# Decoder layer on one core: score maxima and exponentials of two chunks by one instruction across two PSUM banks

## The reference

```python
def xattn(q, ctx):                       # q: (2, 512, 128), ctx: (2, 154, 128)
    qh, kh, vh = heads(q @ Wq + bq), heads(ctx @ Wk + bk), heads(ctx @ Wv + bv)
    logits = einsum('bhqd,bhkd->bhqk', qh, kh) / sqrt(8)
    i, j = arange(512)[:, None], arange(154)[None, :]
    b = (i >= j - 154 + 512)             # query i sees key j only if i >= j + 358
    logits = logits * b - 1e10 * (1 - b)
    return merge(softmax(logits) @ vh) @ Wo + bo
x = layernorm(x + linear_attention(x))
x = layernorm(x + xattn(x, ctx))
x = layernorm(x + expert_ffn(x))
```

## Time and profile before

| | |
|---|---|
| median of 3 runs | 153.23 us (152.84 to 153.42) |
| the profiled execution | 153.2 us |
| its span, first to last instruction | 151.1 us |
| TensorE busy | 139.0 us (92%) |
| VectorE busy | 98.1 us (65%) |
| ScalarE busy | 93.2 us (62%) |
| GpSimd busy | 76.4 us (51%) |
| TensorE's mean granted clock | 0.970 of full speed |

### The profile page before, as it was taken

One profiled execution on the slowest core, in us unless ns is written; L12 is line 12 of the kernel. 1 busy time (PEld: TensorE's weight loads), 2 busy tenths in 40 slices (PEclk: granted clock), 3 DMA queues, 4 the chain that ended last, 5 costly groups with the idle time before them and its releaser, 6 DMA issues.

```text
span 151.1 us, 2620 instructions
## 1 busy us (share of the span) xinstructions
PE 139.0 (92%) x856; PEld 99.4 (66%) x856; DVE 98.1 (65%) x278; ACT 93.2 (62%) x185; POOL 76.4 (51%) x123
## 2 busy tenths in 40 slices
PE   7999998999999699999799599999999999999950
PEld 2679775656666357577468378876887888888620
DVE  0388898989369500556686775774468866776974
ACT  3276635995943542479866766656567566676761
POOL 8600994489349990003453546654365566654000
PEclk9999999999999955999999999999999999999996
DMA  4839984000000000360143033400843345300013
GB/s 119 247 66 297 359 307 153 0 4 4 0 0 4 0 4 8 108 169 25 46 148 127 7 139 131 121 26 25 265 131 116 105 135 128 127 28 0 2 42 97
DMA packets 9625, 14.44 MB, mean 96 GB/s; under 512 B 1662, under 2 KB 4718, under 8 KB 9356
## 3 DMA queue, kind: packets, MB, share of 16 engines
q1 hardware_dynamic: 9324, 13.75, 29.4%
q10 hardware_dynamic: 288, 0.52, 0.9%
HBM read 13.69 MB, written 0.59 MB: 94 GB/s over the span
## 4 chain that ended last, share of the span: by engine, by line
PE 44%; DVE 15%; issue 15%; POOL 13%; DMA 5%; ACT 4%; POOLq 1%; DVEq 0%; ACTq 0%
POOL ek L826 13%; DMA pT<-comb_d 4%; PE bank L428 4%; PE bank L662 3%; PE bank L664 3%; PE bank L663 3%; PE bank L338 3%; PE bank L345 3%; DVE bank L1080 2%; PE bank L481 2%; DVE alo L1086 2%; PE bank L546 2%; PE bank L520 2%; DVE y L898 2%; PE bank L675 2%
## 5 line engine op out<-in xcount | busy, mean ns | idle before, releaser
L826 POOL TENSOR_TENSOR ek<-ek,pT 128x512 f32<-128x512 f32 x30 | 38.7, 1291 | 43.1 <-ACT ek L1119 40.8
L1080 DVE SCALAR_TENSOR_TENSOR bank<-bank,b_sb,ek 128x512 f32<-128x512 f32 x34 | 25.7, 757 | 20.8 <-POOL ek L826 19.2
L1119 ACT ACTIVATE ek<-bank,b_sb 128x512 f32<-128x512 f32 x34 | 23.4, 688 | 15.4 <-PE bank L664 15.3
L662 PE MATMUL bank<-x2hi,w1hi 128*128 128x512 f32 x68 | 27.8, 409 | 3.1 <-DVE alo L1086 3.1
L1119 ACT ACTIVATE stacks<-bank,mult_sb 128x512 fp32r<-128x512 f32 x34 | 23.4, 687 | 7.1 <-DVE bank L1080 5.9
L664 PE MATMUL bank<-x2hi,w1lo 128*128 128x512 f32 x68 | 26.8, 394 | 0.0
L663 PE MATMUL bank<-x2lo,w1hi 128*128 128x512 f32 x68 | 26.7, 392 | 0.0
L1086 DVE SCALAR_TENSOR_TENSOR alo<-bank,mult_sb,stacks 128x512 fp32r<-128x512 f32 x34 | 25.3, 743 | 1.0 <-ACT stacks L1119 0.9
L662 PEld LDWEIGHTS bank<-x2hi,w1hi 128*128 128x128 f32 x68 | 12.8, 188 | 9.0 <-DVE alo L1086 5.0
L664 PEld LDWEIGHTS bank<-x2hi,w1lo 128*128 128x128 f32 x68 | 12.8, 188 | 3.0
L663 PEld LDWEIGHTS bank<-x2lo,w1hi 128*128 128x128 f32 x68 | 12.8, 188 | 2.5
(11 more groups left out here) (189 smaller groups left out, 236.3 us busy)
## 6 DMA issues: line engine op xcount, KB each, us to landing
pT<-comb_d SPq DMA_DIRECT2D x30, 256.0 KB, 3.2
early<-w1T_d SPq DMA_DIRECT2D x1, 1536.0 KB, 7.7
late<-w2T_d SPq DMA_DIRECT2D x1, 1088.0 KB, 5.4
early<-w1T_d SPq DMA_DIRECT2D x1, 640.0 KB, 4.6
early<-xT_d ACTq DMA_DIRECT2D x2, 256.0 KB, 4.4
x_sb<-x_d SPq DMA_DIRECT2D x1, 512.0 KB, 9.8
out_d<-y SPq DMA_DIRECT2D x4, 128.0 KB, 1.8
wA_sb<-wA_d SPq DMA_DIRECT2D x1, 256.0 KB, 3.9
```

The source lines that it names most:

```text
L662: mm(bk[:], w1hi[:, u, c], x2hi[:, s, :], start=True, stop=False)
L826: pool.tensor_tensor(gl[:, n % 2, :], gl[:, n % 2, :], comb_bc[:, s, e % UPL, :], ALU.mult).then_inc(S["gc_ready"], 1)
L1080: dve.scalar_tensor_tensor(out=bank[HBANK[n % 3]][:], in0=bank[HBANK[n % 3]][:], scalar=b1_sb[:, u, 0:1], in1=gl[:, n % 2, :], op0=add_, o ...
L1119: return nc.scalar.activation(out, in_, f, **kw)
```

## The change

The eight PSUM tensors become four of two banks each, and `bank[i]` a view of one half. `maxima` and `probabilities` are called once per pair of chunks and reduce, or exponentiate, both chunks by one instruction that reads both banks; the 128-row part and the 26-row part stay two instructions. Each waits for the second chunk's signal, and every wait on `m_ready` or `p_ready` counts half as many signals.

```diff
-        bank = [ctx.enter_context(nc.psum_tensor(f"bank{i}", [P, 512], F32)) for i in range(8)]
+        banks = [ctx.enter_context(nc.psum_tensor(f"banks{i}", [P, 2, 512], F32)) for i in range(4)]
+        bank = [banks[i // 2][:, i % 2, :] for i in range(8)]
...
+        def two_chunks(view, c):
+            return view.rearrange("p (q r) -> p q r", r=4)[:, c // 2:c // 2 + 2, 2 * (c % 2):2 * (c % 2) + 2]
+        def two_chunks_of(view, c):
+            return view.rearrange("p (q r) n -> p q r n", r=4)[:, c // 2:c // 2 + 2, 2 * (c % 2):2 * (c % 2) + 2, :]
...
-                    pe.wait_ge(S["m_ready"], 2 * (max(m for m in range(n) if sbank(m) == sbank(n + 1)) + 1))
+                    pe.wait_ge(S["m_ready"], max(m for m in range(n) if sbank(m) == sbank(n + 1)) + 1)
...
-                    pe.wait_ge(S["p_ready"], 2 * n)
+                    pe.wait_ge(S["p_ready"], n)
...
             def maxima(n):
                 b, c = n // 8, CHUNKS[n % 8]
-                bk = bank[sbank(n)]
-                dve.wait_ge(S["s_mm"], n + 1)
-                dve.tensor_reduce(mA[:, b, 2 * c:2 * c + 2], bk[:, 0:2 * NS].rearrange("p (h n) -> p h n", h=2), AX.X, ALU.max)                    .then_inc(S["m_ready"], 1)
-                dve.tensor_reduce(mB[0:QB, b, 2 * c:2 * c + 2], bk[0:QB, 2 * NS:2 * NS + 2 * C2].rearrange("p (h n) -> p h n", h=2),
-                                  AX.X, ALU.max).then_inc(S["m_ready"], 1)
+                bk = banks[sbank(n) // 2]
+                dve.wait_ge(S["s_mm"], n + 2)
+                for m, r, c0, w in ((mA, P, 0, NS), (mB, QB, 2 * NS, C2)):
+                    dve.tensor_reduce(two_chunks(m[0:r, b, :], c), bk[0:r, :, c0:c0 + 2 * w].rearrange("p k (h n) -> p k h n", h=2),
+                                      AX.X, ALU.max).then_inc(S["m_ready"], 1)
...
-            for n in range(8):
+            for n in range(0, 8, 2):
                 maxima(n)
             maxima_split(0, 0)
             maxima(8)
             maxima_split(0, 1)
-            maxima(9)
...
-            for n in range(10, 16):
+            for n in range(10, 16, 2):
                 maxima(n)
-                if n == 11:
+                if n == 10:
                     negated_means(1, mv2, rstd2, 1)
...
             def probabilities(n):
                 b, c = n // 8, CHUNKS_T[n % 8]
-                bk = bank[2 + n % 2]
-                act.wait_ge(S["sT_mm"], n + 1)
-                A(pT1[:, b, 2 * c:2 * c + 2, :], bk[:, 0:2 * NS].rearrange("p (h n) -> p h n", h=2), ACT.Exp).then_inc(S["p_ready"], 1)
-                A(pT2[0:C2, b, 2 * c:2 * c + 2, :], bk[0:C2, 2 * NS:2 * NS + 2 * C2].rearrange("p (h n) -> p h n", h=2), ACT.Exp)                    .then_inc(S["p_ready"], 1)
+                act.wait_ge(S["sT_mm"], n + 2)
+                for t, r, c0, w in ((pT1, P, 0, NS), (pT2, C2, 2 * NS, C2)):
+                    A(two_chunks_of(t[0:r, b, :, :], c), banks[1][0:r, :, c0:c0 + 2 * w].rearrange("p k (h n) -> p k h n", h=2), ACT.Exp)\
+                        .then_inc(S["p_ready"], 1)
...
-            for n in range(16):
-                probabilities(n)
+            for n in range(1, 16, 2):
+                probabilities(n - 1)
```

More of the change, by code:

```diff
@@ L502, in max_transposes @@
                 if b:
-                    pe.wait_ge(S["m_ready"], 32)
+                    pe.wait_ge(S["m_ready"], 16)
                 nc.tensor.transpose(bank[6][:, 0:QB], mmB[0:QB, :], ident[0:QB, 0:QB])
@@ L538, in pv @@
             def pv(b, u):
-                pe.wait_ge(S["p_ready"], 2 * (8 * b + 4 * (u // 2) + 4))
+                pe.wait_ge(S["p_ready"], 8 * b + 4 * (u // 2) + 4)
                 pe.wait_ge(S["va_ready"], G + 4 * B)
@@ L706, in _ @@
             pe.wait_ge(S["cT_ready"], 1)
-            pe.wait_ge(S["p_ready"], 32)
+            pe.wait_ge(S["p_ready"], 16)
             pe.wait_ge(S["y2_ready"], 1)
@@ L954, in maxima_split @@
                     return
-                dve.wait_ge(S["m_ready"], 16 * (b + 1))
+                dve.wait_ge(S["m_ready"], 8 * (b + 1))
                 dve.wait_ge(S["c_mm0"], 2)
```

## The result

| | before | after |
|---|---|---|
| runs of the first comparison | 153.23, 152.84, 153.42, 153.20 us | 150.89, 153.42, 150.75, 153.63 us |
| median | 153.21 us | 152.15 us |
| the profiled execution, its span | 153.2, 151.1 us | 150.89, 148.9 us |
| TensorE's mean granted clock in it | 0.970 | 0.983 |

The comparison's ratio is 0.985 (95% interval 0.981 to 0.988); it counts as disturbed, and leaves out, the two runs of the changed kernel above 153 us, which are more than 1.5% above its fastest. The four runs of the changed kernel stand in two groups, though, 2.7 us apart, and the groups are what has to be explained: a change in the work would have moved all four. The median of all four lies 0.7% under that of before, at a time between the groups that no run has.

A forecast was written before the change was run, and what follows sets the result against it. TensorE was taken to bound the cross-attention, except for a 1.36 us gap near 50 us behind router steps and exponentials. Savings of 0.08 (exponentials) and 0.02 (maxima) took 153.2 to 153.1 us; range 149.6 to 153.8.

The forecast's parts named there:

- Exponentials: Cross-attention, ScalarE: a merged pair takes 0.82 us instead of 0.90; the pair of chunks 10 and 11 saves 0.08 us.
- Maxima: Cross-attention, VectorE: a merged pair takes 0.96 us instead of 1.09 but starts 0.11 later, so ends 0.02 us earlier.
- The detour over GpSimd: Earlier maxima start GpSimd's `w1lo` train earlier, and the router steps sharing its ports move along: 0.02 us.
- TensorE's waits: TensorE's waits on the cross-attention maxima: the tightest, chunks 8 and 9, ends at 31.26 against 31.28, so nothing changes.
- The move of chunk 9: Chunk 9's maximum, now ahead of the query correction, adds about 0.4 us but fits into 0.64 us of idle time.
- Sum: TensorE's 1.36 us gap near 50 us shrinks by 0.08 + 0.02 = 0.10 us, and the end moves by the same.
- the second and third rivals: Merged instructions: second bank costs a second instruction, 153.2 to 153.3 us, 15%; two-bank reductions at half rate, 155.7 us, 8%.
- The step that failed: After the gap near 50 us TensorE's chain is unbroken, so the end moves by the gap's 0.10 us.
- The prediction's own sign of being wrong: Wrong if the 6.8 us at clock 0.50 after the gap near 50 us is gone, or a second stretch follows.
- the reading of the strip: Granted-clock strip of the whole kernel: TensorE at full level but for two slices near 55 us and the very end.
- The first rival: TensorE's clock does not fall to 0.50 behind the shortened cross-attention gap near 50 us; 149.7 us; 17%.
- The fourth rival: The clock falls once more, behind the 1.65 us gap at 83.70, costing 3.4 us; 156.5 us; 5%.

The follow-up runs named there:

- exponentials alone: The changed kernel with exponentials merged per pair but maxima per chunk as before; 150.16, 150.87 and four runs from 153.26 to 153.81 us.
- before with the five products: The kernel before with five more identity products in TensorE's gap near 50 us; fifteen of eighteen runs from 149.86 to 150.37 us.
- half a product more: The kernel before with half an identity product (256 columns) more in TensorE's gap near 50 us; median 152.1 us over 12 runs.

## Why the prediction was right, and where it was not

**Exponentials.** 685 and 235 ns were expected and 682 and 231 measured; 0.08 us off the path was expected, and the pair takes 0.79 against 0.90 us, so 0.11. The execution with the exponentials alone shows 0.07 on the path, because its pair started 0.04 us later behind the scores than that of before. By the Trainium skill, "ScalarE: Activation LUTs", section "What ACT_TABLE_LOAD costs", it would have been 0.19; the row was the better guide here.

**Maxima.** 0.96 us a pair was expected and measured. The merged reduction started 0.04 us behind the second mask product, where the sum had put in 0.05 as an estimate. The train started 0.03 us nearer to the mask products where 0.02 was expected, and the router steps moved with it: from `lg` to the shuffle it is 3.10 us, and 49.08 - 45.95 = 3.13 before (the chain there has `45.95 0.29 DVE lg L1005`). The detour over GpSimd is consistent with this, but no run moved the train by more than 0.03 us, so it is not shown by itself. `dl` takes 0.82 us again beside the train, which agrees with what the Trainium skill says of the shared ports ("SBUF — State Buffer", section "SBUF: two separate sides"). In one execution, that of before with the five products at a clock of 0.95, `dl` started at 47.97, just ahead of a step of the train at 47.99, and took 0.21 us. By this one execution it is a step already started that makes `dl` long, not the train as such.

**TensorE's waits.** No gap from 27.48 to 49.66, as expected. The move of chunk 9 cost nothing.

**Sum.** 0.10 expected, 0.13 measured from the scores to TensorE's return, and 0.10 to 0.17 over eight executions. As a statement on the work, the forecast was right, and the second and third rivals are refuted: two banks cost nothing extra.

**The step that failed** is the sentence that behind the gap TensorE's chain is unbroken, so the end moves by the same: it took the profiled execution's clock for that of all executions. The stretch of 6.83 us at 0.50 and the first rise at 5.5 us were one draw of several. The kernel before has runs of 149.5, 151.5, 153.3 and 154 us without any change, and four runs that all fell near 153.2 had hidden it. The first comparison's 1.5% is the difference between two runs of the low group and four of the high one. The prediction's own sign of being wrong, that the stretch at 0.50 is gone, also came true in part: it is half as long in the profile of after, and in other executions it is absent or stands elsewhere. And the reading of the strip, full level but for two slices and the end, missed the slow start, which the strip leaves out.

**The first rival** had the right mechanism, a clock that does not stay down behind this gap, and two errors. It was priced as all or nothing, 3.4 us: the commonest better case is a stretch of 3.41 us at 0.50, worth 1.6 in the chain. And it was conditioned on the change, where the kernel before shows it too. The full 3.0 us exist, but for the gap filled, not shortened by a tenth. Its argument that length alone does not decide holds: a gap of 1.27 us (half a product more) was followed by no fall, one of 1.28 us (exponentials alone) by 3.41 us at 0.50.

**The fourth rival** looked for a second fall at 83.70, and none of the profiles has one there. A second place exists, at the first scores, where TensorE is hardly idle.

**The range**, 149.6 to 153.8, held the median and each of the four runs. It reached that far down because of the first rival. That the first median came out so near to the forecast is partly luck: it is the middle of two low and two high runs, and with a low run in place of a high one it would have been near 150.9. Over all sixteen runs of the changed kernel the median is 152.8, 0.3 us under the forecast.

## What to carry to other kernels

Before costing a change of tenths of a microsecond, ask whether the runs shown are all of one kind: list the mean granted clock of every run, and compare runs only within a group of the same clock. A gap on TensorE that is followed by a stretch at half the clock costs more than its own length; filling it with products that compute nothing, ahead of a wait that is there anyway, gained some twenty times what the merging did (3.0 us of the chain against 0.13). Merging two instructions saves part of what starting one costs, here 0.05 to 0.07 us each, and it counts only on the path.

## What the runs showed of the hardware

A reduction and an activation whose input spans two PSUM banks cost the same per column as within one: 682 ns for 616 columns where 308 took 414, that is 0.87 ns for each added column, and 797 against about 465 ns on VectorE, 1.08. Within one bank, from 52 to 308 columns, it was 0.88 and 1.07 (190 to 465 ns).

TensorE's first nine products took 3.44 us in one execution and 4.02 in another with nothing changed ahead of them. The Trainium skill, "TensorE: Matmul & The Clock Gate", section "What's actually happening", says that how many products run at the lower clock at the start differs from run to run of one kernel; these rows agree.

A gap of TensorE of 1.1 to 1.4 us at the same place was followed by 0, 3.41 or 6.83 us at 0.50 of the clock, and a stretch with next to no idle time, the first scores, by 6.83 us in three executions. Each of these falls came 47.79 or 23.89 us behind the clock's first rise. In one run of before with the five products, the clock was 0.95 from 6.4 to 146 us, and the run took 151.46.
